# A two-layer transformer kernel on one core: a bank and tiles of its own for the first batch's keys, stores part by part, and two batches rotated on ScalarE and GpSimd

## What is computed

```
def rot(t):
    t2 = jnp.stack([-t[..., 1::2], t[..., 0::2]], axis=-1).reshape(t.shape)
    return t * cos + t2 * sin
...
q, k = _rope(q, k)
scores = jnp.einsum('bhqd,bhkd->bhqk', q, k)
probs = jax.nn.softmax(scores, axis=-1)
out = jnp.einsum('bhqk,bhkd->bhqd', probs, v)
```

## Time and profile before

| | |
|---|---|
| median of 3 runs | 981.61 us (981.26 to 983.02) |
| the profiled execution | 982.85 us |
| its span, first to last instruction | 981.0 us |
| mean granted TensorE clock | 0.916 of full |
| PE busy | 831.7 us (85%) |
| DVE busy | 696.9 us (71%) |
| ACT busy | 579.7 us (59%) |
| POOL busy | 461.6 us (47%) |

### The profile page before, as it was taken

The page is one execution under the profiler, slowest core; times in us unless marked ns, Lnnn a source line. Parts: engine busy times, 40 slices in busy tenths (PEclk is TensorE's granted clock), DMA queues, the critical chain, the costliest instruction groups (busy, mean ns, idle before and its releaser), DMA issues. The chain is left out here.

```text
span 981.0 us, 15587 instructions
## 1 busy us (share of the span) xinstructions
PE 831.7 (85%) x4972; PEld 449.9 (46%) x4972; DVE 696.9 (71%) x1454; ACT 579.7 (59%) x923; POOL 461.6 (47%) x607
## 2 busy tenths in 40 slices
PE   4788888998789978998899989988899888799586
PEld 3222232544245515654464544634564557376353
DVE  6888786688678756788678658847877435577574
ACT  2256676575567466866686668546857864443252
POOL 0152144025458535573747367383645763663201
PEclk9558889999899979999999989989999999889688
DMA  7524344354824354446073613680156045010001
GB/s 207 164 92 99 73 99 164 86 161 130 208 52 148 122 165 92 113 123 192 25 214 95 202 28 114 182 247 17 42 179 198 25 147 180 24 39 19 1 12 38
DMA packets 97063, 110.77 MB, mean 113 GB/s; under 512 B 14191, under 2 KB 76783, under 8 KB 95616
## 3 DMA queue, kind: packets, MB, share of 16 engines
q1 hardware_dynamic: 92954, 102.06, 36.6%
q0 software_dynamic: 3584, 7.35, 2.6%
q10 hardware_dynamic: 444, 0.36, 0.1%
HBM read 84.06 MB, written 26.26 MB: 112 GB/s over the span
## 5 line engine op out<-in xcount | busy, mean ns | idle before, releaser
L1459 ACT ACTIVATE probs<-scores 128x1024 f32<-128x1024 f32 x256 | 262.0, 1024 | 116.0 <-PE scores L1077 84.8
L1772 DVE TENSOR_REDUCE negmax<-scores_for_max 128x2 f32<-128x1024 f32 x192 | 234.3, 1220 | 59.0 <-PE scores_for_max L1052 45.8
L1087 PE MATMUL weighted_values<-probs,vaug 128*32 128x512 f32 x1024 | 147.6, 653 | 1.1 <-ACT probs L1459 1.1
L1149 PE MATMUL expert_units<-xt,ring 128*128 128x128 f32 x840 | 122.7, 289 | 13.4 <-DVE mu L1949 5.6
L1077 PE MATMUL scores<-qs,ks 51*128 51x512 bf16 x512 | 106.0, 407 | 32.3 <-ACT probs L1459 27.9
L1149 PEld LDWEIGHTS expert_units<-xt,ring 128*128 128x128 f32 x840 | 105.2, 195 | 56.3 <-issue 47.6
L1052 PE MATMUL scores_for_max<-ks,qs 48*128 48x512 bf16 x384 | 76.8, 396 | 15.8 <-DVE negmax L1772 11.3
L2222 POOL DMA_INDIRECT xs_d<-xbn,rowpos x56 | 55.6, 994 | 50.2 <-DVE rowpos L1905 35.4
L2233 POOL DMA_INDIRECT y<-ys_d,rowpos x56 | 55.4, 989 | 37.9 <-DMA ys_d<-slot_rows 21.4
L1077 PEld LDWEIGHTS scores<-qs,ks 51*128 51x128 bf16 x512 | 25.5, 94 | 103.2 <-ACT probs L1459 64.2
L1768 DVE TENSOR_REDUCE negmax<-scores_for_max 128x1 f32<-128x512 f32 x86 | 56.4, 682 | 7.5 <-PE scores_for_max L1046 3.6
(11 more groups left out here) (325 smaller groups left out, 1666.3 us busy)
## 6 DMA issues: line engine op xcount, KB each, us to landing
ring<-in_experts SPq DMA_DIRECT2D x113, 384.0 KB, 5.2
slot_rows<-xs_d SPq DMA_DIRECT2D x7, 960.0 KB
parts_d<-parts SPq DMA_DIRECT2D x15, 384.0 KB, 2.6
qs<-parts_d SPq DMA_DIRECT2D x14, 384.0 KB
ks<-parts_d SPq DMA_DIRECT2D x14, 384.0 KB
ys_d<-slot_rows SPq DMA_DIRECT2D x21, 256.0 KB
w<-in_L_ffn_w SPq DMA_DIRECT2D x16, 256.0 KB
parts_d<-parts SPq DMA_DIRECT2D x15, 256.0 KB, 2.9
```

The lines of the kernel that those rows point to most:

```text
L1087: last = nc.tensor.matmul(pv[32 * j:32 * j + 32, :], vaug[:, kt, PAIRS * (j // 2) + GP * g + j % 2, :], probs[:, kt % 2, j % 2, j // 2, :] ...
L1149: last = nc.tensor.matmul(dst[:, at], ring[:, q % RING, j, first + f * P:first + (f + 1) * P], xt[:, q % 2, at], start=True, stop=True)
L1459: nc.scalar.activation(probs[:, kt % 2, j, :, :].rearrange("p m s -> p (m s)"), se[:, :], ACT.Exp)\
L1772: V.tensor_reduce(negmax[:, g % 2, :, n], sm[:, :].rearrange("p (m s) -> p m s", m=2), AX, ALU.max, negate=True)\
```

## The change

For the keys of batch 0 the projection goes to the bank `m0`, and its products and sum to the tiles `uz`, `u2` and `nt3` (which lies in `xdn`). The modulation rows that used `m0` go to the bank of the expert units, so the third maximum unit now waits for their copy. Every store of a part is a step of its own, which waits for that part alone; queries and keys are stacked by a step each, batch 0 in two pieces instead of four. For batches 1 and 2 (`COPIED`) the three products on DVE go: ACT copies the bank to `uz` and, with halves swapped, to `u2`, and POOL multiplies both and subtracts. The table of slots is new for all engines and the whole program.

```diff
+COPIED = (1, 2)
...
+        def proj_bank(b, n):
+            return m0 if (b, n) == (0, 1) else m1
+
+        def turned(b, n):
+
+            return (uz, u2, nt3) if (b, n) == (0, 1) else (rot1, rot2, rem)
...
-            def p_store(b, which):
-
-                after_all(sp, ("p_part2", b, which + 1))
+            def p_store(b, which, k):
+
+                after(sp, f"p_part{k}", b, which + 1)
                 stack_loaded(sp, b - 1)
...
+            def p_stack(b, n):
+
+                after(sp, f"p_stored{n}", b, 16 * PARTS)
+                after(sp, "a_sef", b - 2, 32)
+                dst = (qs, ks)[n]
+                for at in ((slice(0, GP), slice(GP, PAIRS)) if b == 0 else (slice(0, PAIRS),)):
...
+                        if u == 2:
+                            pe.wait_ge(s_m1, SM_COPIED)
...
+            def turn(b, n):
+                if b not in COPIED:
+                    return
+                after(act, "p_proj", b, n + 1)
+                after(act, "p_sum", b, n)
+                nc.scalar.activation(uz[:, :], m1[:, :], ACT.Copy)
+                nc.scalar.activation(u2[0:HALF, :], m1[HALF:P, :], ACT.Copy)
+                nc.scalar.activation(u2[HALF:P, :], m1[0:HALF, :], ACT.Copy).then_inc(sig["p_rot"], 1)
...
             def rot(b, n, k):
+                if b in COPIED:
+                    return
...
                 after(pool, "p_rot", b, n + 1)
                 after(pool, "p_part2", b, n)
+                if b in COPIED:
+                    pool.wait_ge(s_rope, 16 * N_ROPE)
+                    first = 4 * COPIED.index(b) + 2 * n
+                    G.tensor_tensor(uz[:, :], uz[:, :], cosT[:, :], ALU.mult).then_inc(sig["p_mul"], 1)
+                    G.tensor_tensor(u2[:, :], u2[:, :], sinT[:, :], ALU.mult).then_inc(sig["p_mul"], 1)
+                    pool.wait_ge(sig["p_mul"], first + 2)
+                    G.tensor_tensor(rem[:, :], uz[:, :], u2[:, :], ALU.subtract).then_inc(sig["p_sum"], 1)
+                    return
```

More of the change, by code:

```diff
@@ L64 @@
     ("P", "split"): [(n,) for n in range(2)],
+    ("P", "turn"): [(n,) for n in range(2)],
     ("P", "split2"): [(n,) for n in range(2)],
     ("P", "split3"): [(n,) for n in range(2)],
-    ("P", "store"): [(n,) for n in range(2)],
+    ("P", "store"): [(n, k) for n in range(2) for k in range(PARTS)],
+    ("P", "stack"): [(n,) for n in range(2)],
     ("P", "silu"): [(L,) for L in range(2)],
@@ L311 @@
-        ("P", "rope"): dict(sp=(3, 7, 18, 19, 20, 21, 22, 23)),
-        ("P", "late"): dict(sp=(8, 9, 12, 13, 26, 27, 28, 29)),
-        ("B", "blank"): dict(sp=(10, 11, 24, 25, 33, 40, 41, 42)),
-        ("P", "second"): dict(sp=(30, 32, 34, 35, 36, 37, 38, 39)),
-        ("P", "store"): dict(sp=(43, 44, 62, 64, 67, 69, 79, 81, 92, 97, 111, 113, 140, 144, 168, 174)),
-        ("P", "stack"): dict(sp=(45, 65, 71, 83, 101, 121, 147, 177)),
-        ("P", "modst"): dict(sp=(47, 48, 49, 50, 51, 52, 53, 54)),
@@ new lines @@
+        ("P", "whhi"): dict(act=(20, 21, 22, 23, 24, 25, 26, 27)),
+        ("P", "hT"): dict(act=(28, 43, 57, 129, 183, 247, 342, 477)),
+        ("P", "small"): dict(act=(29, 30, 31, 32, 33, 34, 35, 36)),
+        ("P", "split"): dict(act=(38, 40, 46, 52, 65, 82, 135, 147, 194, 201, 261, 276, 358, 384, 491, 510), dve=(165,
+        186, 187, 188, 189, 190, 191, 192, 193, 194, 195, 196, 197, 198, 199, 200), pool=(20, 21, 26, 31, 37, 40, 59,
+        64, 74, 77, 109, 114, 153, 165, 217, 225)),
@@ new lines @@
+        ("P", "load"): dict(sp=(14, 42, 59, 87, 104, 127, 153, 184)),
+        ("P", "rope"): dict(sp=(15, 16, 17, 18, 19, 20, 21, 22)),
+        ("B", "blank"): dict(sp=(23, 24, 36, 37, 38, 39, 40, 41)),
+        ("P", "second"): dict(sp=(28, 29, 30, 31, 32, 33, 34, 35)),
+        ("P", "store"): dict(sp=(43, 44, 45, 46, 47, 48, 66, 67, 69, 71, 72, 73, 76, 77, 78, 79, 81, 82, 93, 95, 96,
+        98, 99, 100, 112, 113, 114, 117, 120, 121, 134, 136, 138, 140, 141, 142, 164, 171, 172, 174, 177, 179, 202,
@@ new lines @@
+        203, 205, 209, 211, 213)),
+        ("P", "stack"): dict(sp=(49, 50, 70, 74, 85, 86, 102, 103, 125, 126, 150, 151, 176, 181, 206, 216)),
+        ("P", "modst"): dict(sp=(51, 52, 53, 54, 55, 56, 57, 58)),
+        ("C", "load"): dict(sp=(60, 145, 168, 199, 225, 242, 264, 268)),
+        ("B", "load"): dict(sp=(61, 65, 128, 154, 178, 200, 227, 246)),
+        ("C", "loadd"): dict(sp=(62, 161, 188, 218, 235, 251, 266, 270)),
+        ("C", "loadu"): dict(sp=(63, 156, 183, 214, 231, 247, 265, 269)),
@@ L351 @@
 }
+M0_USES["P", "proj"] = ("p_rot", lambda n: n + 1)
 M1_USES = {
@@ L364, with in_bank @@
 IN_OTHER_BANKS = ("xT", "qk", "hid", "sim", "out", "xT3", "up", "dn")
+def in_bank(uses, stage, step, b, *args):
+    if (stage, step) == ("P", "proj") and (uses is M0_USES) != (b == 0 and args[0] == 1):
+        return False
+    return (stage, step) in uses and not elsewhere(stage, step, b, *args)
 def elsewhere(stage, step, b, *args):
@@ L612, in bank_waits @@
         def bank_waits(uses, b, stage, step, *args):
-            order = [u for u in order_of("pe") if u[:2] in uses and not elsewhere(u[0], u[1], u[3], *u[2])]
+            order = [u for u in order_of("pe") if in_bank(uses, u[0], u[1], u[3], *u[2])]
             at = order.index((stage, step, args, b))
@@ L829, in p_stack @@
[L829 to L841 removed]
+                n = k if which else PARTS - 1 - k
@@ L1541, in hid @@
                         act.wait_ge(s_small, 1)
+                        after(act, "p_sum", COPIED[-1], 2)
                 nc.scalar.activation(hz[:, :], m1[:, :], ACT.Identity, bias=bh[:, c:c + 1])
@@ L1685, in mod_second @@
                 if b == 0 and part == 0:
+                    after(dve, "p_part2", b, 2)
                     dve.wait_ge(s_colm, 3)
@@ L1713, in first_split @@
                     after(dve, "p_rot", b, n + 1)
-                    after(dve, "p_part2", b, n)
-                    V.tensor_tensor(rem[:, :], rot1[:, :], rot2[:, :], ALU.add).then_inc(sig["p_sum"], 1)
+                    one, two, left = turned(b, n)
+                    V.tensor_tensor(left[:, :], one[:, :], two[:, :], ALU.add).then_inc(sig["p_sum"], 1)
             def first_split2(b, n):
@@ L1733, in run @@
                 def run(b):
+                    if (key, b) == ("p", 1):
+                        after(dve, "p_part2", 0, 2)
                     for w in wait:
@@ L1749, in rot @@
             def rot(b, n, k):
+                if b in COPIED:
+                    return
+                got, (one, two, _) = proj_bank(b, n), turned(b, n)
                 if k == 0:
```

384 lines of the change are left out of this document (182 added, 202 removed), and 121 rows, old and new, of the table SLOTS.

## The result

| | before | after |
|---|---|---|
| median | 982.05 us (8 runs, 977.77 to 986.02) | 990.68 us (8 runs, 985.20 to 994.88) |
| ratio, 95% interval | | 1.0083 (1.0050 to 1.0116) |
| span of the profiled execution | 981.0 us | 983.1 us |
| mean granted clock | 0.916 | 0.931 |

The change makes the kernel slower by 0.8%, where 0.2% faster was forecast (2.3 us of 981.61) and the range ended at 986.5. Before itself was measured anew beside every experiment, so only ratios are compared between them.

A forecast was written before the change was run, and what follows sets the result against it. PE was taken to bind from 54 to 70 and 90 to 104 us, DVE between; -1.3 at exponential 17 and -1.0 from the low stretch made -2.3 us, from 981.61 to 979.3, range 973.5 to 986.5.

The forecast's parts named there:

- Scalings ahead of the value copy: At the start, ACT's five scalings now precede the value copy: +0.85 us, between 0 and +1.9.
- Keys with their own bank: Batch 0's keys on DVE: 10.2 us, -1.1; with statistics +1.2 and `wh_lo` +0.7, first reduction at about 38.0, nothing gained.
- Stores part by part: Storing and stacking key parts before the first maxima: 0, covered by DVE's modulation steps; modulation store goes at 38.0.
- POOL ahead of group 0: `w2g` now precedes the splitting of group 0's maxima: `mparts` at 50.5, +2.6 us, bounds 1.4 and 4.5; first exponential 56.8.
- What the rotations give back: Rotations moved from DVE to ACT and POOL: group 2's `mparts` at 79.6, exponential 17 at 87.5, 1.2 to 1.4 us earlier.
- The low stretch: Low clock from 90 to 104 us, exponentials 17 to 24: a fifth of 4.8 us regained, 1.0 us.
- rival 3: Low stretch from 90 us goes altogether, as PE is fed evenly: -6 us in all, 975.6; chance 0.10.
- The later order: New order of steps behind exponential 24: shift carried on; reordered last 120 us count 0, give or take 3 us.
- The first: Rival: POOL's queue decides, `mparts` after 51.5 (group 0) and 83 (group 2), exponential 17 late: +3, 984.6; chance 0.29.
- The second: Rival: PE in written order waits for ACT, whose copies hold exponentials about 1.3 us; later shift nil, 981.6; chance 0.24.

The follow-up runs named there:

- new_then_old_120: The changed kernel with its own order of steps until about 120 us and the old order from there on; 984.04 us, 1.0042 to before.
- no_copies_early_statistics: The changed code with no batch copied, old order except DVE's first steps, batch 1's statistics ahead of the last key parts; 977.37 us, 0.9980 to before.
- maxima_before_pool_work: The changed kernel with the old order behind 120 us, POOL splitting maxima of groups 0 and 2 ahead of other work; 990.25 us, 1.0103 to before.
- new_between_120_and_785: The kernel before with the changed kernel's order of steps between 120 and 785 us alone; 982.30 us, 1.0020 to before.

## Why the prediction was wrong

It forecast -2.3 us, and +8.6 was measured. By the terms above, which are estimates, the start is +0.50% or 4.9 us, and the order behind it +0.44% or 4.3 us, together 9.2.

**Scalings ahead of the value copy: the mechanism right, its size at the edge.** In `new_then_old_120` the last constant landed at 14.68 (14.96 forecast) and the copy came at 15.90, +1.5 and not +0.85, inside the bounds. Not seen at all: the modulation weights, the first thing that PE needs. PE began at 10.4 to 10.9 in 3 of the 14 profiles with the changed start (after among them) and at 6.9 to 7.8 in the others; in the six with the old start it began at 7.4 to 8.6. On the average that is 8.1 and 7.9, so it explains little of the loss, and whether the change makes the late beginnings likelier is not shown.

**Keys with their own bank: 10.2 us forecast, 10.05 measured; last modulation step at 39.90.** Taking the 2.0 us off by which the value copy was later than forecast (17.26 less 14.37 less 0.85), that is 37.9 as forecast, and the first reduction, 39.84, is at 37.8. The error was to book the statistics as +1.2 us of DVE time and no more. Batch 1's chain hangs on them, and they start 2.0 us later against the value copy. `no_copies_early_statistics` has them back ahead of the last key parts, and its first exponential is 2.4 us earlier for it.

**Stores part by part: 0 at the first maxima, right.** The modulation store goes at 39.93, right when its rows are ready. But a store that is a step of its own also stands in SP's queue ahead of the maxima, and there it can hold them (7.63 us in `maxima_before_pool_work`). I had looked only at what it frees.

**POOL ahead of group 0: the times right, less the 2.0 us, the reason only half.** `w2g` at 48.2 (47.6 forecast), `mparts` at 51.0 (50.5), first exponential at 56.4 (56.8); in the three other profiles of this start 56.7 to 57.0. But the forecast had the maxima ready at 49.3 and POOL's list as what holds them. They were ready at about 51.4, as the experiment with the maxima first shows, mainly because DVE waited for PE's work for batch 1 and for a load among them. That the two ends fell together was luck.

**What the rotations give back: this step of the start failed.** The 2.6 us that the forecast rightly had at the first exponential were to be made good by exponential 17, which was to come 1.3 us earlier than before; it came 4.0 us later in after and 7.0 to 8.5 in the three other profiles of this start. The copies take 0.59 to 0.60 and the products 1.26 to 1.28, as priced, and the first products on POOL (45.85 to 49.67) lie beside reductions that keep their 0.6 us each. But "ACT's parts 3.2 us and tokens 2" added durations where the engines wait for each other by turns: less the 2.0, group 2's maxima are split at 82.4 where 79.6 was forecast, and exponential 17 comes at 90.8 where 87.5 was. That exponential 9 would be 5.8 to 7.3 us behind 8 the sum did not contain; the new order of ACT and PE does that, with batch 2's copies or without them. The new order has DVE idle where it was the bound, and PE idle with it: from 70 to 90 us PE is busy 13.98 of 20 us at full clock, where it was 16.96.

**The low stretch: rival 3's condition came true in after, and not reliably.** The clock at 1.00 from 90 to 104 gave back all that had been lost in this one execution. In another of the same start it was at 0.74 from 70 to 90 and at 0.50 from 90 to 104, and before was 8.6 us ahead at exponential 24. The forecast had taken one stretch of one execution for a property of the kernel; the unchanged start also runs without it (`new_between_120_and_785`). A start with both batches copied costs 4.9 us (1.9) in the runs, and 5 us at exponential 37 in the profiles. Which part of the start does it, the copies of batch 2 or the new order of ACT and PE, stays open; so does whether it acts by the lost PE time or by where the clock then falls.

**The later order: counted as 0 give or take 3, measured +4.3.** The sentence that failed is "behind exponential 24 of batch 0 the three big tables follow each other in almost the old order, so a shift there is carried on". Almost the old order is not the old order: with the same code, the new tables behind 120 us alone make the kernel slower by 0.54% (0.22 to 0.87). I had looked for the danger in the last 120 us, where the differences are easiest to see; the fit puts the larger part of the loss between 120 and 450 us, without telling the places apart. Which exchange of steps there does it stays open.

**The rivals.** The first (POOL's queue decides, +3, 984.6) is nearest in sign and place. Its mark for `mparts` of group 0, 51.5, was passed in after (52.98) and in one other profile of this start (51.59), and missed in two (51.43, 51.30); group 2's passed its mark of 83 in all four (83.5 to 84.4). But its remedy, the maxima first on POOL, made the kernel slower, group 0's maxima were not ready any earlier, and GpSimd's products taken away from batch 2 did not make it faster. So POOL's queue is not what decides alone. The second (PE takes its steps in the written order, ACT holds an exponential by about 1.3 us) has the mechanism of exponential 9, with 4.2 to 5.7 us in place of 1.3, and its "later shift is nil" failed with the forecast's. The range ended at 986.5 because the two sources of loss, start and order, were never added.

## What to carry to other kernels

When steps of a chain move from one engine to two others, count the chain's waits and not the engines' sums, and ask of every step that moves back by 1 us of work what hangs on it (here the statistics, booked as 1.2 us, which cost 2.4 at the first exponential). Compare several executions before a stretch of one trace is priced as a property of the kernel. When a table of orders is made anew for a small change, measure the old order behind the change too: here about half of the loss was in the order far behind the code that changed. And before mending an order at the place where the trace shows a wait, look who waits for the step that is pushed back; three such mends here cost 0.6 to 1.2% each.

## What was not expected of the hardware

The clock's second low stretch is not tied to a place in the program. With one and the same work up to 120 us it was absent in one execution, at 73.1 to 76.5 and 79.9 to 90.1 us in another and at 79.5 to 113.6 in a third, and exponential 24 came at 103.5, 106.5 and 113.1. And a level of the whole kernel moved: before took 978.8 to 982.1 us (median) in five measurements and 960.5 in the last, with nothing changed in it. Its own executions show a mean clock of 0.933 in the last one and of 0.920 to 0.923 in the four ahead of it; what moved the clock stays open. Only ratios within one measurement mean anything at the level of 1%.
